# One block for everything: routing by quarters inside the first attention, fixed regions for the experts' rows

## The reference

```python
def layer(x, ctx, g_attention, g_ffn, attention, ffn):
    x = x + tanh(g_attention) * attention(layernorm(x), ctx, ctx)
    return x + tanh(g_ffn) * ffn(layernorm(x))

# x: (32, 128, 128)   ctx: (32, 77, 128)
# attention 0: one head of 128, masked softmax, then a LayerNorm of the context with gamma and beta
scores = (q @ Wq + bq) @ (ctx @ Wk + bk).T / sqrt(128)      # mask == 0 -> -inf
attention0 = layernorm(softmax(scores) @ (ctx @ Wv + bv)) * gamma + beta
# feed-forward 0: the best of 8 experts for each of 4096 rows, plus a shared expert; C = 128, H = 256
idx = argmax(x_ @ router.T)
y  = (silu(x_ @ gate[idx].T) * (x_ @ up[idx].T)) @ down[idx].T
ys = (silu(x_ @ w_gate_s.T) * (x_ @ w_up_s.T)) @ w_down_s.T
ffn0 = y + ys
# attention 1: 16 heads of 8, logit scale, relative position bias, output projection Wo and bo
# feed-forward 1: for each row the one of 8 maps whose signature sign(tile_sigs) scores best
ffn1 = x_ @ W[idx1] + b[idx1]
```

## Time and profile before

| | us |
|---|---|
| median of 3 runs | 618.58 |
| lowest, highest | 616.97, 621.12 |
| the profiled execution | 621.03 |
| its span in the trace | 619.2 |

### The profile page before, as it was taken

One profiled execution on the slowest core, in us unless ns is written; L12 is line 12 of the kernel. 1 busy time (PEld: TensorE's weight loads), 2 busy tenths in 40 slices (PEclk: granted clock), 3 DMA queues, 4 the chain that ended last, 5 costly groups with the idle time before them and its releaser, 6 DMA issues.

```text
span 619.2 us, 14247 instructions
## 1 busy us (share of the span) xinstructions
PE 534.1 (86%) x3643; PEld 339.4 (55%) x3643; DVE 403.0 (65%) x1188; ACT 343.9 (56%) x1013; POOL 367.2 (59%) x740
## 2 busy tenths in 40 slices
PE   0189999769626999989999999999999999999963
PEld 0167777536314666666665565656656566565520
DVE  6138888756103434435888888888888888888731
ACT  0137888531002555528767767677676766767510
POOL 4206677626760555543477776777768777776541
PEclk9989999769677999988999999999999999999965
DMA  7822225401111222210000000000000000000000
GB/s 191 128 78 70 76 74 168 103 1 39 52 51 27 78 76 79 63 35 5 10 11 19 10 17 17 8 17 8 17 15 10 17 8 17 11 10 10 10 5 8
DMA packets 39731, 25.50 MB, mean 41 GB/s; under 512 B 9727, under 2 KB 37025, under 8 KB 39698
## 3 DMA queue, kind: packets, MB, share of 16 engines
q1 hardware_dynamic: 34946, 19.58, 12.4%
q0 software_dynamic: 2272, 4.67, 2.4%
q10 hardware_dynamic: 2480, 0.85, 0.6%
HBM read 15.68 MB, written 10.04 MB: 42 GB/s over the span
## 4 chain that ended last, share of the span: by engine, by line
PE 61%; issue 5%; POOL 4%; another core or an unknown queue 3%; DVE 3%; ACT 1%; DMA 1%; POOLq 0%; SPq 0%; DVEq 0%; ACTq 0%
PE bank L1164 12%; PE bank L1112 10%; PE bank L1103 7%; PE bank L1125 7%; PE bank L1099 3%; POOL routed L781 3%; PE bank L832 3%; PE bank L1136 2%; PE bank L1173 2%; PE bank L792 2%; PE bank L793 2%; PE bank L801 1%; PE bank L1152 1%; PE bank L848 1%
## 5 line engine op out<-in xcount | busy, mean ns | idle before, releaser
L1215 ACT ACTIVATE PRT<-bank 77x512 f32<-77x512 f32 x128 | 74.6, 583 | 18.0 <-PE bank L1112 16.0
L1112 PE MATMUL bank<-cst,SC 128*77 128x128 f32 x512 | 81.0, 281 | 0.2 <-ACT SC L1207 0.2
L1164 PE MATMUL bank<-w,xn3T 128*128 128x512 f32 x128 | 75.7, 675 | 2.5 <-DVE XN L1372 2.0
L1207 ACT ACTIVATE SC<-SC,low 128x77 f32<-128x77 f32 x256 | 67.4, 346 | 1.2
L1112 PEld LDWEIGHTS bank<-cst,SC 128*77 128x77 f32 x512 | 59.6, 150 | 14.5 <-issue 13.9
L781 POOL DMA_INDIRECT routed<-ys,to x39 | 37.2, 953 | 45.4 <-issue 25.4
L1304 DVE TENSOR_TENSOR SC<-bank,biasQ 128x616 f32<-128x616 f32 x64 | 51.1, 799 | 15.3 <-PE bank L1103 15.3
L1125 PE MATMUL bank<-PRT,VP 77*32 77x128 f32 x1024 | 54.5, 285 | 0.7 <-ACT PRT L1215 0.7
L1372 DVE TENSOR_TENSOR XN<-bank,OH 128x512 f32<-128x512 f32 x64 | 44.3, 692 | 15.1 <-PE bank L1164 11.8
L1103 PE MATMUL bank<-KB,QT 32*128 32x308 f32 x256 | 51.6, 480 | 0.0
L1311 DVE TENSOR_REDUCE top<-SC 128x8 f32<-128x616 f32 x64 | 50.5, 789 | 1.1
(11 more groups left out here) (222 smaller groups left out, 1295.7 us busy)
## 6 DMA issues: line engine op xcount, KB each, us to landing
sorted_x<-blank SPq DMA_DIRECT2D x10, 258.0 KB, 4.0
xs<-sorted_x SPq DMA_DIRECT2D x39, 64.5 KB
X<-in_x SPq DMA_DIRECT2D x4, 512.0 KB, 7.6
wgu<-in_wgu SPq DMA_DIRECT2D x16, 128.0 KB
y<-routed SPq DMA_DIRECT2D x32, 64.0 KB, 1.8
out<-res SPq DMA_DIRECT2D x32, 64.0 KB, 1.6
ctxT<-in_ctxT SPq DMA_DIRECT2D x16, 77.0 KB, 1.9
mask<-in_mask SPq DMA_DIRECT2D x16, 77.0 KB, 1.9
```

What stands on the lines that cost most here:

```text
L1112: last = nc.tensor.transpose(bP[c % 2][0:SK, j * 128:j * 128 + 128], SC[u][:, c * HG + j, :], ident)
L1164: nc.tensor.matmul(bF[:, :], xn3T[u][:, :], w2[:, k * HT:(k + 1) * HT, :], start=True, stop=True).then_inc(s["f"], 1)
L1207: last = nc.scalar.activation(SC[u][:, head, :], SC[u][:, head, :], ACT.Exp, bias=low[u][:, head:head + 1])
L1215: nc.scalar.activation(PT[c % 2][:, :], bP[c % 2][0:SK, :], ACT.Copy if c * HG < HH else ACT.Exp).then_inc(s["pTs"], 1)
```

## The change

- The set-up and `attend_0` lose their blocks: the whole kernel is one block (`everything`). Each engine runs attention 0's list, then the feed-forward's, then `attend_1`'s, with semaphores alone between them. Attention 0's turns are written out instead of looped (`written_out`), with larger lags.
- Small weights are joined into a few arrays (`wa`, `wb`, `rows`, `wc`): five loads on ACT's queue instead of 18. SP loads X in pieces of 2, 6, 12 and 12 batches with the first pairs' context and mask between them, then `wide_qk`, and one of 12 `late` loads after each further pair.
- Raw rows of X are transposed (`rows_T`); ACT's normalising pass over X and POOL's `nb0` go. The mean is taken out of `wqT` once (`centre`), and the inverse deviation is multiplied in where DVE adds mask and bias (`masked`). The mask goes in through a bf16 matmul with the identity.
- U's bank is now freed by ACT, which writes the normalised context (`normed`) and for that waits for POOL's `inv_std0`; DVE multiplies by gain and adds the residual later.
- `norm1` writes XN directly. POOL's copy, the second copy of the transposed rows and the copy of the logits go.
- The experts get fixed regions of `sorted_x`, so that a row's slot needs no total counts. Each quarter of eight batches is routed as soon as its logits are there (`route`, `ranked`, `slots`), and POOL scatters batches 0 to 11 from inside attention 0's list (`moved`), the other 20 behind it.
- Blank rows are no longer written over all of `sorted_x` beforehand. SP writes 128 spare rows behind the last row of each expert once the counts are known, at addresses that it loads into a register, and loads each tile from an address that it looks up likewise.
- The gates' scaling of weights moves into DVE's feed-forward list, between the shared expert's products. The values' bias of attention 1 is folded into `bo1` by one matmul.
- `SC` and `sum4` of `attend_1` lie where the experts' weights were; some semaphores are joined.

```diff
+def written_out(n, stages):
+
+    first = min(lag for _, lag in stages)
+    for turn in range(n + max(lag for _, lag in stages) - first):
+        for stage, lag in stages:
+            item = turn - (lag - first)
+            if 0 <= item < n:
+                stage(item)
...
+def everything(nc, sb, sem, sems, bank, a, out, m):
+    f = feed_forward_0(nc, sb, sem, sems, bank, a, m)
+    g = attend_1(nc, sb, sem, sems, bank, out, m, f)
+    h = attend_0(nc, sb, sem, sems, bank, a, m, f)
...
+        def _(sp):
+            h["sp_program"](sp)
+            f["sp_program"](sp, h["n_late"])
+            g["sp_program"](sp)
...
+    pair = lambda g: slice(PAIR * g, PAIR * g + PAIR)
+    piece_of = lambda g: next(k for k in range(len(PIECES) - 1) if PAIR * g + PAIR <= PIECES[k + 1])
...
+    def sp_program(sp):
+        def rows(k):
+            sp.dma_start(X[:, PIECES[k]:PIECES[k + 1], :],
+                         a["x"][PIECES[k]:PIECES[k + 1]].rearrange("b s d -> s b d")).then_inc(s_x[k], 16)
+
+        def load(g):
+            wait(sp, s["mkr"], g - 5)
+            wait(sp, s["v"], g - 5)
+            sp.dma_start(ctxT[g % 6][:, :], a["ctxT"][:, g, :]).then_inc(l_ctx[g % 6], 16)
+            wait(sp, s["mb"], g - 2)
+            sp.dma_start(mask[g % 3][:, :, :], a["mask"][:, pair(g), :]).then_inc(l_mask[g % 3], 16)
+
+        rows(0)
+        load(0)
+        rows(1)
+        load(1)
+        rows(2)
+        load(2)
+        rows(3)
+        sp.dma_start(m["wide_qk"], bass.AP(tensor=a["table"].tensor, offset=128,
+                                           ap=[[a["table"].shape[1], NH], [-1, 128], [1, SK]])).then_inc(m["s_window"], 16)
+        for g in range(3, NG):
+            load(g)
+            if g - 3 < n_late:
+                sp.dma_start(*late[g - 3]).then_inc(s_late, 16)
+        for dst, src in late[NG - 3:]:
+            sp.dma_start(dst, src).then_inc(s_late, 16)
+        sp.wait_ge(m["s_window"], 16)
+        sp.dma_start(m["biasQ"][:, :, :], m["wide_qk"].rearrange("h q k -> q h k")).then_inc(m["s_bias"], 16)
+
...
+        def rows_T(g):
+            if g == 0 or piece_of(g) != piece_of(g - 1):
+                pe.wait_ge(s_x[piece_of(g)], 16)
+            wait(pe, s["xTs"], g)
+            wait(pe, s["wh"], 2 * ((g - 11) // (QB // PAIR)) + 1)
+            for b in range(PAIR):
+                last = nc.tensor.transpose(bXT[:, b * 128:b * 128 + 128], X[:, PAIR * g + b, :], ident)
+            last.then_inc(s["xT"], 1)
...
+            nc.tensor.matmul(bMK[:, 0:PK], wqk[:, :], ctxT[g % 6][:, :], start=True, stop=True)
+            if g == 0:
+                pe.wait_ge(m["s_wb"], 16)
+                pe.wait_ge(s["w0"], 4)
+            nc.tensor.matmul(bMK[:, PK:2 * PK], wk1, ctxT[g % 6][:, :], start=True, stop=True)
+            nc.tensor.matmul(BIAS, uqB[:, :], ctxT[g % 6][:, :], start=True, stop=False)
+            nc.tensor.matmul(BIAS, ones[0:1, :], c0row[:, :], start=False, stop=False)
+            pe.wait_ge(s["mb"], g + 1)
+            nc.tensor.matmul(BIAS, identb[:, :], mb[g % 2][:, :, :].rearrange("p b k -> p (b k)"),
+                             start=False, stop=True).then_inc(s["mkr"], 1)
...
+        def scores(g):
+            wait(pe, s["sm"], g)
+            pe.wait_ge(s["xTs"], g + 1)
+            pe.wait_ge(s["mk"], g + 1)
+            for b in range(PAIR):
+                last = nc.tensor.matmul(bSC[:, b * SK:(b + 1) * SK], xT[g % 2][:, b, :], M[g % 2][:, b * SK:(b + 1) * SK],
+                                        start=True, stop=True)
+            last.then_inc(s["sc"], 1)
...
+        def weigh(g):
+            pe.wait_ge(s["pTs"], g + 1)
+            pe.wait_ge(s["v0"], g + 1)
+            wait(pe, s["z"], g)
+            for b in range(PAIR):
+                last = nc.tensor.matmul(U[:, b, :], PT[g % 2][:, b, :], V0[g % 2][:, b, :], start=True, stop=True)
+            last.then_inc(s["u"], 1)
...
+        def ranked(q):
+            pe.wait_ge(s["cum"], q + 1)
+            nc.tensor.matmul(place(q), ones[:, :], upto[q % 2][:, :, 1:QB + 1], start=True, stop=False)
+            nc.tensor.matmul(place(q), tri, QH[q % 2][:, :, 1:QB + 1], start=False, stop=True).then_inc(s["rk"], 1)
...
+        written_out(NG, [(norm1_T, 7), (rows_T, 1), (values, 3), (weigh, 4), (keys, 0), (probs_T, 3), (scores, 1), (ranks, 8), (logits, 7)])
+        pe.wait_ge(s["cum"], NQ)
+        nc.tensor.matmul(bLG[:, 0:E], ones[:, :], upto[(NQ - 1) % 2][:, :, QB], start=True, stop=True).then_inc(f["s_count"], 1)
+        ranked(NQ - 1)
...
+        def keys(g):
+            act.wait_ge(s["mkr"], g + 1)
+            wait(act, s["sm"], g - 1)
+            nc.scalar.activation(M[g % 2][:, :], bMK[:, 0:PK], ACT.Identity, bias=m0[:, 0:1], scale=D ** -0.5)
+            nc.scalar.activation(K1T[:, pair(g), :], bMK[:, PK:2 * PK].rearrange("p (b k) -> p b k", b=PAIR),
+                                 ACT.Identity, bias=cols[:, 3:4])
+            nc.scalar.activation(bias[g % 2][:, :, :].rearrange("p b k -> p (b k)"), BIAS, ACT.Copy).then_inc(s["mk"], 1)
...
+        def values_1(g):
+            act.wait_ge(s["v0"], g + 1)
+            src = bV[0:SK, :].rearrange("p (b l d) -> p b l d", b=PAIR, l=2)
+            nc.scalar.activation(V1[:, pair(g), :], src[:, :, 1, :], ACT.Copy).then_inc(s["v1"], 1)
...
+        def normed(g):
+            act.wait_ge(s["inv"], g + 1)
+            wait(act, s["zg"], g - 1)
+            for b in range(PAIR):
+                last = nc.scalar.activation(z[g % 2][:, b, :], U[:, b, 0:D], ACT.Identity, bias=nr[g % 2][:, b:b + 1],
+                                            scale=ru[g % 2][:, b:b + 1])
+            last.then_inc(s["z"], 1)
...
+        written_out(NG, [(values_1, 3), (norm1, 6), (probs_T, 3), (keys, 0), (normed, 4), (exps, 2), (rows_T, 0), (norm1_T, 6)])
...
+        stats(0)
+        dve.wait_ge(s["act0"], 2)
+        nc.vector.tensor_scalar(uqB[:, :], ones[:, :], uq[:, 0:1], D ** -0.5, ALU.mult, ALU.mult).then_inc(s["w0"], 1)
...
+        stats(1)
+
+        def mask_bias(g):
+            dve.wait_ge(l_mask[g % 3], 16 * (g // 3 + 1))
+            wait(dve, s["mkr"], g - 1)
+            nc.vector.tensor_scalar(mb[g % 2][:, :, :], mask[g % 3][:, :, :], 0.0, NEG, ALU.is_equal, ALU.mult).then_inc(s["mb"], 1)
+            if 2 <= g + 1 < len(PIECES) - 1:
+                stats(g + 1)
...
+        def masked(g):
+            dve.wait_ge(s["sc"], g + 1)
+            dve.wait_ge(s["rs"], piece_of(g) + 1)
+            wait(dve, s["ex"], g - 1)
+            for b in range(PAIR):
+                i = PAIR * g + b
+                last = nc.vector.scalar_tensor_tensor(out=sm[g % 2][:, b, :], in0=SCO[:, b, :], scalar=rstd0[:, i:i + 1],
+                                                      in1=bias[g % 2][:, b, :], op0=ALU.mult, op1=ALU.add)
+            last.then_inc(s["sm"], 1)
...
+        def residual(g):
+            u = g % 2
+            dve.wait_ge(s["z"], g + 1)
+            if g == 0:
+                dve.wait_ge(s["w0"], 7)
+            nc.vector.tensor_tensor(z[u][:, :, :], z[u][:, :, :], spread(gain), ALU.mult).then_inc(s["q"], 1)
+            dve.wait_ge(s["xb"], g + 1)
+            dve.wait_ge(s["q"], 4 + g)
+            wait(dve, s["inv1"], g - 1)
+            nc.vector.tensor_tensor(X[:, pair(g), :], z[u][:, :, :], xb[u][:, :, :], ALU.add).then_inc(s["zg"], 1)
...
+        def route(g):
...
+            dve.wait_ge(s["lg"], g + 1)
+            then(nc.vector.tensor_reduce(best[:, :], logit, AX.X, ALU.max))
...
+            nc.vector.tensor_tensor_scan(flat(upto[q % 2]), segments, flat(own), 0.0, ALU.mult, ALU.add).then_inc(s["cum"], 1)
...
+            dve.wait_ge(s["rk"], q + 1)
+            nc.vector.tensor_tensor(where[:, :, :], place(q), QH[q % 2][:, :, 1:QB + 1], ALU.mult).then_inc(s["wh"], 1)
...
+        written_out(NG, [(values_0, 5), (attend_stats, 6), (residual, 7), (route, 10), (masked, 3), (slots, 10), (mask_bias, 0)])
...
+    def scatter(pool, b):
+        pool.wait_ge(s["slot"], b // QB + 1)
+        nc.gpsimd.indirect_dma_start(sorted_x, bass.IndirectOffsetOnAxis(ap=slot[:, b:b + 1], axis=0),
+                                     XN[:, b, :], None).then_inc(f["s_scat"], 16)
...
+        def shifted(g):
+            if g + 2 < len(PIECES) - 1:
+                invert(g + 2)
+            if g == 0:
+                pool.wait_ge(s["w0"], 7)
...
+        def inv_std0(g):
+            u = g % 2
+            pool.wait_ge(s["umv"], g + 1)
+            wait(pool, s["z"], g - 1)
+            nc.gpsimd.tensor_tensor(vr[u][:, :], es[u][:, :], es[u][:, :], ALU.mult).then_inc(s["iv0"], 1)
+            nc.gpsimd.tensor_tensor(nm[u][:, :], mv[u][:, :, 0], minus[:, 0:1].to_broadcast([128, PAIR]), ALU.mult).then_inc(s["iv0"], 1)
+            pool.wait_ge(s["iv0"], 4 * g + 2)
...
+            nc.gpsimd.tensor_tensor(nr[u][:, :], nm[u][:, :], ru[u][:, :], ALU.mult).then_inc(s["inv"], 1)
...
+        def moved(g):
+            if g >= QB // PAIR:
```

(26 more changed lines are left out.)

953 lines of the change are left out of this document (423 added, 530 removed).

## The result

The changed kernel takes 593.43 us (median of 4 runs, 589.44 to 595.35) against 617.78 for the kernel before, measured beside it; the ratio is 0.9593, with a 95% interval from 0.9526 to 0.966. It is 24 us faster. I had forecast 585 with a range of 577 to 604, which is 34 us faster. The profiled execution took 593.72 us, its span is 591.8.

What follows compares the result with a forecast made beforehand. The question was when the first expert tile starts: 160.5 instead of 194.5 us (attention 0 and set-up -8.8, shared stage 35.7 instead of 63.9, gap 7.0 instead of 4.0). Span 585.2, forecast 585 us, range 577 to 604.

Steps and rivals of the forecast that it cites:

- rival 1: Shared expert: the burst of scatters makes the engines stand still again, experts start at 175, 600 us in all; chance 0.25.
- rival 2: Attention 0: turns a microsecond longer through small delays in the loop of U's bank, 16 us, 600 us in all; chance 0.18.
- Landmark: Set-up: DVE's first statistics of U, marking the filled pipeline, at 28.5 us instead of 44.2, gain 15.7.
- Attention from there: Attention 0 from the first statistics of U to the last `inv_std1`: 89.3 us, ending at 117.8.
- route turn: Attention 0's turns in which DVE routes a quarter and PE waits in `ranked`: 1.4 us for each of three.
- Gap to the shared expert: From attention 0's end to PE's first shared matmul: 7.0 us instead of 4.0, so that matmul is at 124.8.
- shared expert: From first shared matmul to first expert tile: 35.7 us instead of 63.9, set by PE, not the scatter; experts at 160.5.
- Last stage: From the first expert matmul to the end: taken as unchanged at 424.7 us.
- rival 3: Attention 0: each of eight scatters in POOL's turns stops the other engines, say 7 us each, 640 us in all; chance 0.04.
- rival 4: Faster start: `wide_qk` doesn't delay mask 3 and the routing turns cost nothing, 575 us in all; chance 0.06.
- The rule against it: Attention 0: DVE's two-SBUF-input residual operations hold POOL, 0.42 us each, 10.9 us over 13 turns, about 595; not adopted.
- stand-still: Kernel before, 157 to 188 us: DVE and ACT idle about 20 us on nothing named, PE doing 11.9 us of work.

Runs made afterwards that it cites:

- route_first: The changed kernel with `route` moved ahead of the statistics of U and the residual in VectorE's list: 591.32 us, ratio 0.9545.
- both: The changed kernel with `wide_qk` loaded behind the tenth pair's loads and `route` ahead of the statistics of U: 600.66 us, ratio 0.9582.
- second trace: The kernel before, unchanged, profiled once more: 622.86 us, span 621.0.

## Why the prediction was right, and where it was off

The direction and the places were right: set-up shorter, attention longer, the large gain at the shared expert, TensorE and not the scatters setting the start of the experts. The size was less so: 24 us were gained of the 34 forecast, and 593.43 lies just outside the forecast's own range of 578 to 592, where I had put rivals 1 and 2. The difference of 8.8 us is made of these terms:

- **Landmark, +3.9.** 32.40 against 28.5, inside the bounds of 22 to 34. That `wide_qk` delays the fourth mask is shown by moving the load: 20.42 without a wait instead of 25.43, and a landmark of 28.04. I had put the mask at 24 and the landmark 4.5 us behind it. That the mask was nearly right is in part luck: X was in at 18.6 and not at 13, and `wide_qk` landed 14.5 us behind its issue at 10.55, not 11.5 us behind X. The rest was 7 us, since in the first turns VectorE waits for another mask and for TensorE's banks (0.75, 1.34 and 1.13 us). With the load moved the rest is 7.6, so a landmark near 28.5 is what the kernel gives without the delay that I had priced in.
- **Attention from there, +3.1** (92.4 against 89.3). Two errors against each other: the three routings cost about 11 us instead of 4.2 (4.0, 4.4 and, in the drain, 2.7), and the other turns gave 3.7 back. The plain turn was 4.48 instead of 4.9: I took the removed rank-one matmul at 0.74, but in the turn of the earlier trace rows the four steps of scores (L472 and L473, from 76.84 to 78.30) fill 1.46 us, and the four matmuls of L452 that replace them take 0.40. The route turn was mis-sized the other way: I said 1.4 (bounds 0.5 and 2.5), and it is 4. I had named the statistics and the residual ahead of `route` in VectorE's list, but priced only VectorE's own operations. Left out altogether was that TensorE's granted clock falls to its lower level (1.2 GHz) behind a 2.56 us wait, so that what follows is stretched as well. `route_first` shows the first, since the wait for the counts goes with the edit, and L429's 1.61 the second.
- **Gap to the shared expert, -0.7** (6.3), **shared expert, -1.3** (34.4): as forecast.
- **Last stage, +1.6.** 426.3 against 424.7. In the twelve traces beside this one and the forecast's own it is 425.2 to 430.3, and none of their edits touches this part, so this is spread.
- **Profiled execution against median, +2.2.** I carried over that the profiled run had been 2.45 above the median; this time it was 0.3 above.

**Rivals.** 1 did not come in the changed kernel's two traces. Where it did come, its price for the stage was near: 50 us from the first shared to the first expert matmul, against 52.2 and twice 57.0 with scatters inside attention. That "both" took 600.66 us like the rival's 600 is chance, since it carries two edits that save time. 2 came in part: two full turns are longer by 4.0 and 4.4 us and the third routing costs 2.7 in the drain, not sixteen turns by one. 3 is out, at 0.5 us per scatter. 4 is out as well: `wide_qk` does delay the mask, the routing turns cost 11 us, and even with the load moved U is at 28.04 and not at 22.

**The rule against it.** I dismissed it on a misreading: in the kernel before, L628 never ran beside POOL's small operations, only beside its copy to XN (L674, 0.39 to 0.41 us), so their 0.19 was no test. In the changed kernel two of POOL's operations run beside VectorE's residual and take 0.28 and 0.29 us instead of 0.19 (63.21 and 63.72); each begins 0.16 to 0.19 us into a VectorE operation and ends 0.05 us behind it. The power starts behind the pair, at 0.70; the one time that it ran beside, it took 0.81 instead of 0.71 (43.29). So the contention is there, at 0.2 us a turn and not 0.84, and in plain turns TensorE covers it. The page (the Trainium skill, SBUF — State Buffer, Who interferes with whom) is right in kind; by these rows it's worth 3 us of POOL's time at most.

**What I read wrongly about the kernel before.** I took the stand-still's removal as part of the 34 us. The second trace has none and starts its experts at the same time. The gain comes from the routing order: the first scatter used to start 16 us behind the last nb with 32 to go, and now POOL goes on 0.4 us behind it with 25 to go. Two runs take this apart: with the routing done once, the first scatter starts 10.8 us behind the last nb ("once", ahead of its stand-still), and with all scatters behind attention the experts start 7 us later. Of the 27.4 us between the two spans, 27.2 lie between the last nb and the first expert matmul (20.7 against the second trace of the kernel before); the shorter start gives 11.8, and attention takes 10.0 back. Which part of the new set-up gives the 11.8 was not tested.

## To carry to other kernels

In a stretch that is full of work, price a wait by all that is queued ahead of what it waits for, and add the stretch at the lower clock behind it. A hole in a trace is worth only what lies behind it: ask what would end last if it were gone, and take a second trace before a forecast rests on it. A large strided load belongs behind the small loads that the pipeline starts on, and moved work must be followed to its new place.
